# Gated cross-attention block on one core: the opening put in another order, tile 0 normalised by VectorE, first z in one block

## The chip, the cores and the metric

The kernel runs on 1 core of a Trainium2 chip. The metric is the device time of one execution in microseconds. Engines are named TensorE (PE in the rows; PEld its weight loads; PEldq its queue's own instructions), VectorE (DVE), ScalarE (ACT), GpSimd (POOL) and SyncE (SP, which here only issues DMAs).

## What is computed

x is 2048 tokens of 512 numbers. Each token belongs to one of four experts by its token id, and an expert is one 512 x 512 matrix, ctx[e], used three times. Then a feed-forward block with 1536 inner columns and weights rounded to 8-bit floats follows. Shapes and helper code are left out:

```python
e_id = minimum(clip(itok, 0, 24999) // 6250, 3)
n = layernorm(x)                                  # per token, eps 1e-5
for e in range(4):
    z = n @ ctx[e].T
    h = silu(z) * z
    y = where(e_id == e, h @ ctx[e].T, y)
x = x + tanh(g_xattn) * y
w8 = lambda w: w.astype(float8_e4m3fn).astype(float32)
n = layernorm(x)
fuse = silu(n @ w8(gate_w) * gate_scale) * (n @ w8(up_w) * up_scale)
x = x + tanh(g_ffn) * (fuse @ w8(down_w) * down_scale)
```

## The kernel before

**Stages.** The opening (0 to 17 us) sorts the tokens by expert with one-hot products (lines 971 to 1006 on VectorE, 1396 to 1419 on TensorE), so that 16 tiles of 128 sorted tokens follow each other. GpSimd gathers each tile of x by its row numbers (`gather`, L524). Then 19 steps (16 tiles, and one more for each of the three tiles at which the expert can change) run the expert part: z = tile times matrix (`product_z`), h = z silu(z) on VectorE (`product_h`), h turned by four small TensorE products (`turn_h`, L1391), y = h times matrix (`product_y`), and the sum into x on VectorE (`add_expert`, L1112). Which expert and which tile a step works on is read from three words of a table, `walk` (`load_word`, L370). From 135 us on, four groups of four tiles run the feed-forward block; its 36 weight slabs are rounded during the steps, mostly by GpSimd (L620, L623).

**Precision.** Every operand of z and y is split in a 16-bit high and low part. z has 12 products of 512 columns: high x high and high x low for each of four chunks of 128 rows, and low x high for four. The same holds for y (8 at L1483, 4 at L1487). The high part of a turned tile is a copy by ScalarE (`x_high`, L728), the low part is a difference by VectorE (`x1_low`, L1083).

**Expert 0.** Its matrix is turned by TensorE in the opening (`first_turn`, L1405) into four PSUM banks, MT_FIRST. ScalarE makes the high parts (`first_high`, L705), VectorE the low parts (`first_low`, L1012). The other three matrices are split on ScalarE, VectorE (L1172) and GpSimd (`expert_low(2)`, L595) and turned by DMA. Each matrix is scaled by a power of two taken from its sum of squares: ScalarE sums (`squares`), TensorE adds over the partitions, and VectorE computes in `expert_scales` (L939 to L951) one column for each expert: m_scale, m_inv, z_scale, h_scale and m_inv2; `expert_y_scales` makes y_scale from m_inv2 and m_inv. `hot_steps` compares the expert of each step with 0 to 3; `zh_tables` multiplies this one-hot by the scales and adds over the experts, which gives one scale a step for silu and for h.

**Layer norm.** For each tile VectorE takes statistics (`tile_stats`, L1062), `aggregate` (L1071) and `prepare` (L965, L967), GpSimd raises to the power -1/2 and multiplies (`ln_scalars`, L532, L535), ScalarE normalises into the only buffer xn (`normalise`, L723), and TensorE turns it (`turn_x`, L1391).

**Order.** Each engine has its own list of instructions, written out by hand, and works it in order; semaphores are the only coupling. What stands late in a list is late whatever it waits for. TensorE's list in the opening is: two chunks of first_turn, the sort products, the sum for expert 0, two chunks of first_turn, 16 products whose result nobody reads (L1425), turn of tile 0, the three words, then step 0: eight products of z, turn of tile 1, the sum for experts 1 and 2 (L1463, L1465), four products of z. A step s from 1 on is: turn of tile s+1, z(s), turn of h(s-1), y(s-2), with y(0) and y(1) ahead of the turn of h. Banks: Z alternates between 0 and 5, turned tiles between 2 and 4, turned h is bank 1, y bank 3, small things bank 6.

## Time and profile before

| | us |
|---|---|
| median of 3 runs | 401.99 (401.97 to 402.08) |
| the profiled execution | 401.0 |
| its span | 399.3 |
| TensorE busy | 378.4 (95%) |
| VectorE busy | 224.1 (56%) |
| ScalarE busy | 185.5 (46%) |
| GpSimd busy | 163.2 (41%) |

The page splits the span in 40 equal slices of 10 us; a digit is the busy share of TensorE in a slice in tenths, the second line is the clock that it was granted:

```profile
PE   3889899999999999999999999999999999999992
PEclk9999999999999999999999999999999999999997
```

Only the first slice, those from 10 to 50 us, and the last are below 9 tenths: the first 50 us are the part of the kernel with which the change deals. Of the chain of work that ended last, 79% of the span is TensorE. Times are counted from the start of the span.

### The profile page before, as it was taken

What the parts mean: (1) busy time and instruction counts of PE and PEld (TensorE: products, weight loads), DVE (VectorE), ACT (ScalarE), POOL (GpSimd) and SP (SyncE); (2) the same over time, 40 slices, a digit from 0 to 9 for tenths busy, and PEclk for the clock granted to TensorE, in tenths of its full rate; (3) what the DMA queues carried; (4) which work ended last, traced back from release to release, by engine and by line L of the source; (5) the groups of instructions that cost most, each with busy time, mean ns of one, the idle gap of its engine ahead of it and who ended that gap; (6) DMA issues with size and microseconds to landing.
All of it is one profiled execution on the core that took longest, in us unless ns stands there. A gap on an engine that the chain in (4) does not pass through costs nothing.

```text
span 399.3 us, 6082 instructions
## 1 busy us (share of the span) xinstructions
PE 378.4 (95%) x1920; PEld 184.3 (46%) x1920; DVE 224.1 (56%) x467; ACT 185.5 (46%) x297; POOL 163.2 (41%) x204
## 2 busy tenths in 40 slices
PE   3889899999999999999999999999999999999992
PEld 2444455555545544444444444444444444444460
DVE  5878979998787696787434222224222225322253
ACT  3779457789778428693432222222222222222220
POOL 4778889999999831411008000006200004400003
PEclk9999999999999999999999999999999999999997
DMA  7698684354445340760002000001100000200002
GB/s 263 190 313 183 127 214 113 88 108 114 101 115 112 80 105 2 178 167 0 0 2 79 28 0 0 2 0 54 53 0 0 0 0 28 79 0 2 0 0 105
DMA packets 40075, 29.99 MB, mean 75 GB/s; under 512 B 31192, under 2 KB 31216, under 8 KB 40048
## 3 DMA queue, kind: packets, MB, share of 16 engines
q1 hardware_dynamic: 37488, 21.26, 21.4%
q0 software_dynamic: 2560, 8.39, 6.1%
q8 instruction: 14, 0.23, 0.2%
q14 instruction: 13, 0.11, 0.1%
HBM read 18.11 MB, written 4.19 MB: 56 GB/s over the span
## 4 chain that ended last, share of the span: by engine, by line
PE 79%; DVE 10%; ACT 3%; issue 3%; POOL 2%; DMA 1%; SPq 1%; DVEq 0%; ACTq 0%; POOLq 0%
PE bank L1551 36%; PE bank L1565 17%; PE bank L1467 11%; PE bank L1483 7%; PE bank L1391 3%; PE bank L1487 3%; PE bank L1425 1%; DMA X<-x2rows 1%; DVE xs L1112 1%; DVE stats L1062 1%; DVE W L1278 1%; DVE xs L1372 1%; DVE row_hot L997 1%; DVE X L1369 1%; DVE cs L1289 1%
## 5 line engine op out<-in xcount | busy, mean ns | idle before, releaser
L1551 PE MATMUL bank<-X,W 128*128 (+1 forms) x752 | 170.0, 379 | 0.1
L1551 PEld LDWEIGHTS bank<-X,W 128*128 128x128 bf16 x752 | 73.5, 98 | 88.8 <-ACT late_norms L879 0.6
L1289 DVE SCALAR_TENSOR_TENSOR cs<-bank,up_mul,cs 128x512 f32<-128x512 f32 x47 | 35.3, 751 | 107.1 <-PE bank L1551 102.4
L1565 PE MATMUL bank<-W,cs 128*128 128x512 bf16 x376 | 89.0, 379 | 0.5 <-ACT W L762 0.5
L837 ACT ACTIVATE cs<-bank,gate_mul 128x512 f32<-128x512 f32 x47 | 32.2, 684 | 75.5 <-PE bank L1551 75.5
L844 ACT ACTIVATE cs<-cs 128x512 f16<-128x512 f32 x47 | 29.5, 628 | 79.8 <-DVE cs L1289 79.7
L676 POOL TENSOR_TENSOR xs<-xs,X 128x512 f32<-128x512 f32 x12 | 15.3, 1275 | 125.2 <-DVE X L1369 124.9
L1565 PEld LDWEIGHTS bank<-W,cs 128*128 128x128 f16 x376 | 36.6, 98 | 44.0 <-issue 0.5
L1467 PE MATMUL bank<-M,X 128*128 (+1 forms) x228 | 52.5, 379 | 2.1 <-ACT X L728 1.5
L1315 DVE TENSOR_TENSOR cs<-cs 128x512 f16<-128x512 f32 x47 | 33.7, 716 | 31.4 <-ACT cs L844 31.4
L1483 PE MATMUL bank<-M,hTh 128*128 (+1 forms) x152 | 35.9, 378 | 1.6 <-DVE xs L1112 1.6
L682 POOL DMA_INDIRECT out<-xs,order x16 | 16.7, 1046 | 49.2 <-DVE xs L1372 45.9
L1467 PEld LDWEIGHTS bank<-M,X 128*128 (+1 forms) x228 | 22.2, 98 | 28.1 <-issue 2.9
L623 POOL TENSOR_TENSOR W<-w_sum,w_big 128x512 bf16<-128x512 f32 x21 | 27.1, 1293 | 1.6
L620 POOL TENSOR_TENSOR w_sum<-ws,w_big 128x512 f32<-128x512 f32 x21 | 26.7, 1271 | 0.7
L532 POOL TENSOR_TENSOR ln_tab<-prep,ln_half 128x1 f32<-128x1 f32 (+1 forms) x26 | 16.6, 638 | 19.1 <-DVE prep L967 18.9
L786 ACT ACTIVATE silu_z<-bank,z_step 128x512 f32<-128x512 f32 x18 | 12.3, 686 | 22.2 <-PE bank L1467 20.1
L636 POOL TENSOR_TENSOR x2rows<-x2n,x2rows 128x512 f16<-128x512 f32 x16 | 19.5, 1222 | 7.3 <-ACT x2n L739 7.3
L1483 PEld LDWEIGHTS bank<-M,hTh 128*128 128x128 f16 x152 | 13.6, 97 | 16.6 <-issue 2.6
L747 ACT ACTIVATE w_big<-ws 128x512 f32<-128x512 f32 x36 | 21.3, 627 | 0.0
L1062 DVE BATCH_NORM_STATS2 stats<-xs 128x6 f32<-128x512 f32 x31 | 20.7, 683 | 0.0
L1487 PE MATMUL bank<-M,hTl 128*128 (+1 forms) x76 | 19.5, 379 | 0.0
(172 smaller groups left out, 385.6 us busy)
## 6 DMA issues: line engine op xcount, KB each, us to landing
ws<-in_L_ffn_gate_w SPq DMA_DIRECT2D x12, 256.0 KB, 2.6
ws<-in_L_ffn_up_w SPq DMA_DIRECT2D x12, 256.0 KB, 3.2
ws<-in_L_ffn_down_w SPq DMA_DIRECT2D x12, 256.0 KB, 2.9
cs<-in_ctx SPq DMA_DIRECT2D x2, 1024.0 KB, 6.7
X<-in_ctx SPq DMA_DIRECT2D x2, 1024.0 KB
xs<-in_x,order POOLq DMA_INDIRECT x16, 4.2
dsc<-in_L_ffn_down_scale SPq DMA_DIRECT2D x1, 256.0 KB
X<-x2rows SPq DMA_TRANSPOSE x16, 3.1
```

Of the source, the lines that this page charges most:

```text
L620: g.tensor_tensor(w_sum[:], ws[:, slot], w_big[:, slot], ALU.add).then_inc(sum_done, 1)
L623: g.tensor_tensor(dst, w_sum[:], w_big[:, slot], ALU.subtract).then_inc(q_done, 1)
L837: a.activation(sg[:, c % 2, :], GATE[c % 2][:], ACT.Silu, scale=gate_mul[:, c:c + 1]).then_inc(sg_done, 1)
L844: a.activation(fuse_part(g, c, 0), fuse[:, c % 2, :], ACT.Copy).then_inc(fh_done, 1)
L1062: return v.bn_stats(stats[:, slot, which, :], xs_tile(tile))
L1289: v.scalar_tensor_tensor(out=fuse[:, c % 2, :], in0=UP[c % 2][:], scalar=up_mul[:, c:c + 1], in1=sg[:, c % 2, :], op0=ALU.mult, op1=ALU.mu ...
L1315: v.tensor_tensor(fuse_part(g, c, 1), fuse[:, c % 2, :], fuse_part(g, c, 0), ALU.subtract).then_inc(fl_done, 1)
L1467: ins = t_.matmul(Z[lo % 2][:], lhs, rhs, start=(n == 0), stop=(n == 3 * KC - 1))
L1483: t_.matmul(Y[:], hTh[:, lo % 2, k * P:(k + 1) * P], expert_block(e, part, k), start=(k == 0 and part == 0), stop=False)
L1487: ins = t_.matmul(Y[:], hTl[:, lo % 2, k * P:(k + 1) * P], expert_block(e, 0, k), start=False, stop=(k == KC - 1))
L1551: ins = t_.matmul(dst[c % 2][:].rearrange("p (t i) -> p t i", t=TPG), w, x2_group(g, part, k), start=(k == 0 and part == 0), stop=(k == KC ...
L1565: ins = t_.matmul(ACC[t][:], fuse_part(g, c, part)[:, t * P:(t + 1) * P], W8[:, down_slab(c), :], start=(c == 0 and part == 0), stop=(c == ...
```

## The change

On ScalarE, `normalise(0)` goes. On VectorE, a TENSOR_SCALAR with mean and factor as scalars makes xn of tile 0 instead, between the low part of chunk 1 and the statistics of tile 1; the low parts of chunks 2 and 3 come behind the statistics of tile 1. On TensorE the first word is loaded ahead of the turn of tile 0, the second and third in steps 3 and 4 behind the turn of h. The first z has the order high x high (four), high x low (four), low x high (four), waits for the low parts only ahead of the second four, and isn't interrupted; the turn of tile 1 and the sum for experts 1 and 2 follow it. The turned chunks 0 and 2 of expert 0 exchange their banks, so that bank 0, in which the first z is built, is free once chunk 0 is split. In step 2 the turns of the two scale rows and the sum for expert 3 go ahead of y(0). On VectorE, m_inv2 is computed in `expert_y_scales`, with a wait behind it; in step 2 `add_expert(0)` goes ahead of the scales of expert 3, the tables follow these at once, and the y scale comes behind h_low(1). A second copy of the one-hot, HOT, is written to PSUM (bank 7), and `zh_tables` reads that one.

```diff
@@ -192,12 +192,13 @@
         Z = [bank[0], bank[5]]
         XT = [bank[2], bank[4]]
         HT, Y, M0_SUM, SMALL = bank[1], bank[3], bank[4], bank[6]
-        MT_FIRST = [bank[5], bank[7], bank[0], bank[1]]
+        MT_FIRST = [bank[0], bank[7], bank[5], bank[1]]
         ACC = [bank[0], bank[1], bank[2], bank[3]]
         GATE = [bank[5], bank[7]]
         UP = [bank[6], bank[4]]
 
         M_SUM = 192
+        HOT = bank[7][:, 0:E * STEPS].rearrange("p (e s) -> p e s", e=E)
 
 
         consts = sem("consts")
@@ -228,6 +229,7 @@
         msum_done = sem("msum_done")
         mchain = sem("mchain")
         mscale_done = sem("mscale_done")
+        minv2_done = sem("minv2_done")
         mT_done = sem("mT_done")
         mhi_done = sem("mhi_done")
         stats_done = sem("stats_done")
@@ -767,7 +769,6 @@
             squares(1, 0, KC, 1, 1)
             first_high()
             squares(2, 0, KC // 2, 2, 2)
-            normalise(0)
             act.wait_ge(params_in, 64)
             a.activation(tgx[:], gx[:], ACT.Tanh).then_inc(tanh_done, 1)
             a.activation(tgf[:], gf[:], ACT.Tanh).then_inc(tanh_done, 1)
@@ -947,8 +948,8 @@
                                      ALU.logical_shift_left), mchain, mcount)
                 link(v.reciprocal(m_inv[:, c], m_scale[:, c]), mchain, mcount)
                 v.tensor_scalar(z_scale[:, c], m_inv[:, c], 1.0 / X_SCALE, None, ALU.mult)
-                v.tensor_scalar(h_scale[:, c], m_scale[:, c], 2.0 ** -24 / X_SCALE, None, ALU.mult)
-                v.tensor_tensor(m_inv2[:, c], m_inv[:, c], m_inv[:, c], ALU.mult).then_inc(mscale_done, 1)
+                v.tensor_scalar(h_scale[:, c], m_scale[:, c], 2.0 ** -24 / X_SCALE, None,
+                                ALU.mult).then_inc(mscale_done, 1)
 
             def expert_y_scales(i, lo, hi):
 
@@ -958,6 +959,8 @@
                     v.tensor_scalar(tgx24[:], tgx[:], 2.0 ** 24, None, ALU.mult).then_inc(gates_done, 1)
                     dve.wait_ge(gates_done, 1)
                 dve.wait_ge(mscale_done, 2 + i)
+                v.tensor_tensor(m_inv2[:, c], m_inv[:, c], m_inv[:, c], ALU.mult).then_inc(minv2_done, 1)
+                dve.wait_ge(minv2_done, 1 + i)
                 v.scalar_tensor_tensor(out=y_scale[:, c], in0=m_inv2[:, c], scalar=tgx24[:, 0:1], in1=m_inv[:, c],
                                        op0=ALU.mult, op1=ALU.mult).then_inc(ys_done, 1)
 
@@ -1051,7 +1054,10 @@
             prepare(0, 0, 1)
             dve.wait_ge(sort_v, chained[0])
             v.tensor_copy(walk[:], e_words[:]).then_inc(walk_done, 1)
-            first_low(range(1, KC))
+            first_low([1])
+            dve.wait_ge(ln_chain, 1)
+            v.tensor_scalar(xn[:], xs[:, 0, :], mv[:, 0, 0, 0:1], ln_tab[:, 0, 0, 0:1], ALU.subtract,
+                            ALU.mult).then_inc(xn_done, 1)
 
             def slab_big(n, slot):
 
@@ -1086,15 +1092,16 @@
             dve.wait_ge(gathered[1], 32)
             tile_stats(1, 0, 1).then_inc(stats_done, 1)
             aggregate(1, 1, 0, 1)
+            first_low(range(2, KC))
             x1_low(0)
 
             def zh_tables(i, experts, steps):
 
                 n = steps.stop - steps.start
                 dve.wait_ge(mscale_done, 2 + i)
-                dve.wait_ge(step_hot_done, 1)
+                dve.wait_ge(step_hot_done, 2)
                 for part, scales in enumerate((z_scale, h_scale)):
-                    ins = v.tensor_tensor(step_sel[:, part, 0:experts, steps], step_hot[:, 0:experts, steps],
+                    ins = v.tensor_tensor(step_sel[:, part, 0:experts, steps], HOT[:, 0:experts, steps],
                                           scales[:, 0:experts].unsqueeze(2).to_broadcast([P, experts, n]), ALU.mult)
                 ins.then_inc(step_sel_done, 1)
                 dve.wait_ge(step_sel_done, 1 + i)
@@ -1187,6 +1194,9 @@
 
             def hot_steps():
                 v.tensor_tensor(step_hot[:], e_of[:, 0:STEPS].unsqueeze(1).to_broadcast([P, E, STEPS]),
+                                iota_q[:, 0:E].unsqueeze(2).to_broadcast([P, E, STEPS]),
+                                ALU.is_equal).then_inc(step_hot_done, 1)
+                v.tensor_tensor(HOT, e_of[:, 0:STEPS].unsqueeze(1).to_broadcast([P, E, STEPS]),
                                 iota_q[:, 0:E].unsqueeze(2).to_broadcast([P, E, STEPS]),
                                 ALU.is_equal).then_inc(step_hot_done, 1)
 
@@ -1212,9 +1222,9 @@
                     x1_low(3)
                 if lo == 2:
                     round_stats(1, 1)
+                    add_expert(0)
                     expert_scales(E - 1, E)
-                    expert_y_scales(1, E - 1, E)
-                    add_expert(0)
+                    zh_tables(1, E, slice(E - 1, STEPS))
                 if lo == 3:
                     expert_low(3)
                     h_low(s - 1, lo - 1)
@@ -1233,7 +1243,7 @@
                     add_expert(s - 2)
                     ffn_norms(0, 2)
                 if lo == 2:
-                    zh_tables(1, E, slice(E - 1, STEPS))
+                    expert_y_scales(1, E - 1, E)
                     v.tensor_copy(gs[:], SMALL[:, 160:160 + IC])
                     v.tensor_copy(us[:], SMALL[:, 176:176 + IC]).then_inc(scales_done, 1)
                 if lo in (5, 6):
@@ -1425,6 +1435,8 @@
                 t_.matmul(XT[0][:], row_hot[:, 0, :], row_hot[:, 0:KC, :].rearrange("p c i -> p (c i)"),
                           start=True, stop=True)
             pe.wait_ge(order_done, 1)
+            words = walk_words(pe)
+            load_word(t_, words, 0)
             pe.wait_ge(xn_done, 1)
             transpose4(XT[0], xn, xT_done)
 
@@ -1434,14 +1446,13 @@
                     return M[:, e, part, k, :]
                 return M[:, ds(e, 1), part, k, :].rearrange("p a f -> p (a f)")
 
-            words = walk_words(pe)
-
             def z_operands(s, lo):
 
                 e = expert_of(words, s) if lo else 0
                 tile = (s - e) & (TILES - 1)
                 return e + 1, [(x_tile(tile, lhs, k), expert_block(e, rhs, k))
-                        for lhs, rights in ((0, (0, 1)), (1, (0,))) for k in range(KC) for rhs in rights]
+                        for lhs, rights in (((0, (0, 1)), (1, (0,))) if lo else ((0, (0,)), (0, (1,)), (1, (0,))))
+                        for k in range(KC) for rhs in rights]
 
             def turn_x(tile):
                 if tile >= 2:
@@ -1450,20 +1461,18 @@
                 transpose4(XT[tile % 2], xn, xT_done)
 
             def product_z(s, lo, matrices, operands):
-                pe.wait_ge(m_ready, matrices)
+                if lo:
+                    pe.wait_ge(m_ready, matrices)
+                else:
+                    pe.wait_ge(mhi_done, KC)
                 pe.wait_ge(xhi_done, min(s + 1, TILES))
                 if lo >= 2:
                     pe.wait_ge(h_done, s - 1)
                 for n, (lhs, rhs) in enumerate(operands):
+                    if lo == 0 and n == KC:
+                        pe.wait_ge(m_ready, 1)
                     if n == 2 * KC:
                         pe.wait_ge(xlo_done, min(s + 1, TILES))
-                    if lo == 0 and n == 2 * KC:
-                        turn_x(1)
-                        pe.wait_ge(ssq_done, 4)
-                        t_.matmul(SMALL[:, M_SUM + 1:M_SUM + E - 1], ones32[:], part_ssq[:, 1:E - 1], start=True,
-                                  stop=False)
-                        t_.matmul(SMALL[:, M_SUM + E - 2:M_SUM + E - 1], ones32[:], part_ssq[:, E:E + 1], start=False,
-                                  stop=True).then_inc(msum_done, 1)
                     ins = t_.matmul(Z[lo % 2][:], lhs, rhs, start=(n == 0), stop=(n == 3 * KC - 1))
                 ins.then_inc(z_done, 1)
 
@@ -1493,12 +1502,15 @@
                 if 1 <= lo < E:
                     turn_x(s + 1)
                 product_z(s, lo, *z_next[0])
+                if lo == 0:
+                    turn_x(1)
+                    pe.wait_ge(ssq_done, 4)
+                    t_.matmul(SMALL[:, M_SUM + 1:M_SUM + E - 1], ones32[:], part_ssq[:, 1:E - 1], start=True,
+                              stop=False)
+                    t_.matmul(SMALL[:, M_SUM + E - 2:M_SUM + E - 1], ones32[:], part_ssq[:, E:E + 1], start=False,
+                              stop=True).then_inc(msum_done, 1)
                 if E <= lo < TILES - 1:
                     turn_x(s + 1)
-                if lo in (2, 3):
-                    product_y(s - 2, lo - 2)
-                if lo >= 1:
-                    turn_h(s - 1, lo - 1)
                 if lo == 2:
                     pe.wait_ge(params_in, 64)
                     pe.wait_ge(mscale_done, 2)
@@ -1506,14 +1518,20 @@
                               stop=True)
                     t_.matmul(SMALL[:, 176:176 + IC], us_rows[:], ident[0:IC, 0:IC], is_transpose=True, start=True,
                               stop=True)
-                for n in squared_of(s - 1, lo - 1) if lo >= 1 else ():
-                    norms(n, n, n % 2, SMALL, KC * n)
-                if lo < STEPS - 1:
-                    z_next[0] = z_operands(s + 1, lo + 1)
                 if lo == 2:
                     pe.wait_ge(ssq_done, E + 1)
                     t_.matmul(SMALL[:, M_SUM + E - 1:M_SUM + E], ones32[:], part_ssq[:, E - 1:E], start=True,
                               stop=True).then_inc(msum_done, 1)
+                if lo in (2, 3):
+                    product_y(s - 2, lo - 2)
+                if lo >= 1:
+                    turn_h(s - 1, lo - 1)
+                for n in squared_of(s - 1, lo - 1) if lo >= 1 else ():
+                    norms(n, n, n % 2, SMALL, KC * n)
+                if lo in (3, 4):
+                    load_word(t_, words, lo - 2)
+                if lo < STEPS - 1:
+                    z_next[0] = z_operands(s + 1, lo + 1)
                 if lo >= 4:
                     product_y(s - 2, lo - 2)
 
@@ -1527,8 +1545,6 @@
                     ins = t_.matmul(out_col, sq[:, slot, j * P:(j + 1) * P], ones[:, 0:1], start=True, stop=True)
                 ins.then_inc(norm_done, 1)
 
-            for i in range(WORDS):
-                load_word(t_, words, i)
             z_next = [z_operands(0, 0)]
             for s in range(STEPS):
                 step(s, s)
```

## Rows read from the trace of the kernel before

**Rows 1.** Windows view, one stage: length, then busy us of each engine.

```profile
80.00:110.00 30.00, 29.99 (x184) 16.55 (x183) 25.79 (x52) 25.07 (x44) 28.27 (x30) 1.00 0.47 108
```

**Rows 2.** Waits of TensorE: line, awaited, us in total, times, longest.

```profile
PE bank L1483 <- DVE xs L1112: 1.6, 3, 1.0
...
PE bank L1565 <- ACT W L762: 0.5, 1, 0.5
```

**Rows 3.** Timeline of TensorE: start, us, line, operation, [idle before <- releaser].

```profile
11.82 5.65 PE L1425 MATMUL bank<-row_hot 128*128 128x512 f16 x16
...
17.31 0.60 PE L1391 MATMUL bank<-ident,xn 128*128 128x128 f32 x4
...
19.37 1.89 PE L1467 MATMUL bank<-M,X 128*128 128x512 f16 x8 [1.46 <-ACT X L728]
...
21.09 0.60 PE L1391 MATMUL bank<-ident,xn 128*128 128x128 f32 x4
...
21.89 1.02 PE L1467 MATMUL bank<-M,X 128*128 128x512 f16 x4
...
46.47 0.66 PE L1391 MATMUL bank<-ident,h 128*128 128x128 f32 x4 [1.33 <-DVE h L1185]
...
55.71 2.75 PE L1467 MATMUL bank<-M,X 128*128 x12
```

**Rows 4.** Timeline of VectorE, 15 to 46 us.

```profile
15.11 2.06 DVE L1012 SCALAR_TENSOR_TENSOR M<-bank,m_scale,M 128x512 f16<-128x512 f32 x3
...
18.59 0.68 DVE L1083 TENSOR_TENSOR X<-bank,X 128x512 f16<-128x512 f32 x1
...
22.36 0.69 DVE L1083 TENSOR_TENSOR X<-bank,X 128x512 f16<-128x512 f32 x1 [1.87 <-issue]
...
34.90 0.16 DVE L939 TENSOR_SCALAR m_sum<-bank 128x1 f32<-128x1 f32 x1 [0.32 <-PE bank L1515]
...
35.99 1.02 DVE L951 TENSOR_TENSOR m_inv<-m_inv 128x1 f32<-128x1 f32 x1
...
37.04 1.07 DVE L961 SCALAR_TENSOR_TENSOR y_scale<-m_inv,tgx 128x1 f32<-128x1 f32 x1
...
38.04 0.74 DVE L1112 SCALAR_TENSOR_TENSOR xs<-bank,y_step,xs 128x512 f32<-128x512 f32 x1
...
39.96 0.46 DVE L1097 TENSOR_TENSOR step_sel<-step_hot,z_scale 128x64 f32<-128x64 f32 x1
...
40.94 0.16 DVE L1237 COPY gs<-bank 128x12 f32<-128x12 f32 x1
...
41.09 0.41 DVE L1059 TENSOR_SCALAR w_big<-w_big 128x512 f32<-128x512 f32 x1
...
45.67 0.74 DVE L1185 SCALAR_TENSOR_TENSOR h<-bank,h_step,silu_z 128x512 f32<-128x512 f32 x1
```

**Rows 5.** Timeline of ScalarE, 16 to 23 us.

```profile
16.09 0.81 ACT L723 ACTIVATE xn<-xs,ln_tab 128x512 f32<-128x512 f32 x1 [1.10 <-POOL ln_tab L535]
...
17.95 0.60 ACT L728 ACTIVATE X<-bank 128x512 f16<-128x512 f32 x1 [0.86 <-PE bank L1391]
...
22.22 0.80 ACT L723 ACTIVATE xn<-xs,ln_tab 128x512 f32<-128x512 f32 x1
```

**Rows 6.** TensorE's queue by source line: count, ns min/median/max, first and last start.

```profile
L370 PEldq TENSOR_LOAD <-walk x3: 304/324/496, 17.1 to 18.6; - x3
...
L1467 PEldq FUSED_REGOPS  x26: 46/46/83, 53.6 to 61.8; - x26
```

**Rows 7.** Timeline of GpSimd, 15 to 41 us.

```profile
15.20 0.58 POOL L532 TENSOR_TENSOR ln_tab<-prep,ln_half 128x1 f32<-128x1 f32 x1 [0.51 <-DVE prep L967]
...
20.87 0.58 POOL L532 TENSOR_TENSOR ln_tab<-prep,ln_half 128x1 f32<-128x1 f32 x1
...
35.84 4.50 POOL L595 TENSOR_TENSOR W<-X,W 128x512 f16<-128x512 f32 x4 [0.29 <-issue]
...
40.29 0.56 POOL L532 TENSOR_TENSOR ln_tab<-prep,ln_half 128x1 f32<-128x1 f32 x1
```

## The prediction

> **What bounds the kernel now.** First the windows view, for how full TensorE is in each stage: 29.99 of 30 us busy between 80 and 110 [rows 1]. Most of the span is therefore TensorE's own work, none of which the change touches: a saving has to come from an idle stretch of TensorE, or from the 16 useless matmuls ahead of the first tile. Then its waits: in the opening 1.46 us on ScalarE's copy of the first turned tile and 1.33 us on h of step 3 (in brackets behind the instruction that waited [rows 3]), 1.6 us in three waits for a sum into x by VectorE, of which 1.0 stands before y of step 1 and about 0.5 near 141 us, and 0.5 on a slab near 169 us [rows 2]. The timeline shows what stands ahead of each. The last two waits of the opening are one story: VectorE goes from one instruction to the next without a pause from 34.90 to 46.41, and TensorE turns h of step 3 at 46.47, right behind it [rows 3, 4]. From there TensorE is full, so the end of the kernel moves as y of step 2 (47.13, behind those four turns) moves. That instant is what I forecast.
>
> **Tile 0 normalised by VectorE.** ScalarE now makes xn from 16.09 to 16.90 [rows 5]. The 16 filler matmuls run from 11.82 to 17.47, and the turns of tile 0 begin at 17.31, as the last filler drains [rows 3]. The change leaves the 16 alone, so an earlier xn is hidden by them: worth 0. Cover lost: none, since xn on VectorE is due by 17.3. It waits for the first of GpSimd's two table instructions (15.20 and 0.58 [rows 7], so 15.8), follows one chunk of first_low (2.06/3 = 0.69 us, from 15.11), and costs 0.41 (the 128x512 f32 TENSOR_SCALAR of L1059) to 0.74 us (a SCALAR_TENSOR_TENSOR of that size) [rows 4]: it ends between 16.3 and 16.6. I take 0.41, the same operation, though nothing depends on it.
>
> **First z.** Between the copy of turned tile 0 (ends 18.55) and z (19.37) lie 0.8 us in which TensorE's queue loads the three words of the walk: they start from 17.1 to 18.6, (18.6 - 17.1)/2 = 0.75 us each [rows 3, 5, 6]. Two move to steps 3 and 4; the first moves ahead of the wait for xn. Whether it then delays the turns depends on how far that queue runs ahead. The address work for a z whose matmuls begin at 55.71 [rows 3] is done from 53.6 [rows 6], some 2 us ahead; and walk is written just before the first_low of 15.11. Cost 0, at most the 0.75 if it had to wait for the fillers. The Trainium skill ("TensorE: Matmul & The Clock Gate", Specifications) gives TensorE's queue as 64 deep; by it the 16 fillers all fit in the queue, and the load is hidden too. So z starts at about 18.7. Its first four products need high parts alone and end at 19.6. The low parts of chunks 2 and 3 now follow tile 1's statistics on VectorE: these start between 16.6 and 17.17 (where 15.11 + 2.06 let them start before), take 1.42 with their aggregate and prepare (17.17 to 18.59 [rows 4]), then 2 x 0.69 gives 19.4 to 20.0; x1_low(0) adds 0.6. The other eight products run at 0.22 each from there: z ends at 21.4 (21.3 to 21.8), against 22.9 before (1.02 from 21.89 [rows 3]).
>
> **What is late next.** z(0) is consumed by silu(0), which stands behind x_high(1) and normalise(2) on ScalarE, and these hang on turn_x(1). That began at 21.09 in the middle of z and now stands behind the whole of it: 21.3 to 21.6. So the gain of 1.5 us on z ends here, and tile 1 comes 0.05 to 0.4 us later; I take 0.1. Besides, tile 2's statistics are now behind two chunks and x1_low(0) on VectorE: its prepare ends about 21.4, and GpSimd's pow, which began at 20.87 [rows 7], begins near 21.5 and gives ln_tab near 22.5. normalise(2), at 22.22 [rows 5], waits for that, so z(1) comes about 0.4 late. GpSimd's gathers 5 and 6 behind it slip by 0.6 too; they are wanted by statistics after 30 us, which covers that. Z(1)'s delay is mostly hidden again: ScalarE's next steps (the 2 us copy of expert 1, x_high(2), normalise(3)) hang on the scales of experts 1 and 2, behind x1_low(1) on VectorE (22.36 [rows 4]), plus 0.1 and less 0.07 for the m_inv2 taken out. I carry +0.1 on ScalarE's chain (0 to 0.4), and with it on GpSimd's expert_low(2), which starts at 35.84 because ScalarE's scaled rows do. VectorE itself, without a pause from 23 us on, gets the second one-hot (0.15), m_inv2 with its wait in the y scales (0.2) and the 0.1: it reaches the end of round_stats(1) 0.4 late, at 34.9.
>
> **Steps 2 and 3.** The sum of squares of expert 3 is taken three us earlier, so VectorE's wait of 0.32 us [rows 4] goes. add_expert(0) goes ahead of the scales: x1 of tile 0 is ready at 35.6 instead of 38.78, and the 1.0 us that TensorE waits for it [rows 2] goes. That gain is then lost at the next wait, for h of step 3, unless VectorE comes earlier as well. There the four GpSimd instructions of expert_low(2), 4.50/4 = 1.12 us each from 35.84 to 40.34 [rows 7], decide. m_inv2 took 1.02 us and y_scale 1.07 for one column, and ended at 37.01 and 38.11, where GpSimd's first and second instruction ended [rows 4, 7]; each waited for GpSimd. The Trainium skill ("SBUF — State Buffer", Who interferes with whom) says the same: an instruction with two SBUF inputs waits for a GpSimd one that reads SBUF, one with an input in PSUM doesn't; by that rule the PSUM copy frees step_sel of the 0.46 against 0.22 [rows 4], and leaves m_inv2 and y_scale to pay. They are moved, not freed. In the new order VectorE has from 34.9: add_expert 0.66, seven small ones 1.1, the tables 0.95, product_h(2) 0.66, h_low(1) 0.6, and m_inv2 is issued at 38.9. That is inside GpSimd's third instruction (38.2 to 39.3), y_scale falls into the fourth, and ends at 40.34 + 0.1 = 40.45, later than in the old order. Behind y_scale VectorE had 46.41 - 38.04 = 8.37 us of work; of it add_expert, product_h, h_low and the tables, 40.94 - 38.04 = 2.90, now go before. So h of step 3 ends at 40.4 + 0.1 + 5.47 = 45.95. If w_big, which took 0.41 us at 41.09, is held by GpSimd's pow (40.29, 0.56 us), 0.45 more: 46.4. Middle 46.2, that is 0.2 earlier than 46.41.
>
> **The moved words.** Word 1 is loaded in step 3, and TensorE idles anyway for h of step 3 one z and one turn later: 0; that idle (1.33 us before, more now) is the cover. Word 2 is loaded between the turns of h(3) and y(2), just behind that wait, where the queue has had no time to run ahead. The turns take 0.66 [rows 3], the load 0.75: 0.05 to 0.3 exposed, I take 0.15.
>
> **Sum.** -0.2 + 0.15 = about 0. The profiled execution took 401.0 us (399.3 span and 1.7 around it), 1.0 under the median of 401.99, so the difference is put on the median: 401.99 - 0.05, 401.9. Its own range: -0.46 (nothing held, load hidden) with the opening's -0.1, to +0.3 (w_big held, load exposed) with +0.3: 401.4 to 402.6.
>
> **Rivals.** (1) The change does nothing that the end sees, TensorE's gaps merely trade places: 402.0. For it speaks the filler cover and the merge at h(3); it differs from the forecast by its reason. (2) The shift is kept and the late waits go too. 0.5 + 0.5 us are left after 120 us [rows 2]; they rest on VectorE and ScalarE chains whose phase against GpSimd may change. With 0.2: 401.99 - 0.2 - 0.95 = 400.85. Against it: those chains follow TensorE. (3) m_inv2 is issued before GpSimd's second instruction ends (38.2): y_scale ends 1.12 earlier, 401.9 - 1.1 = 400.8. It needs VectorE 0.7 us quicker than worked out. (4) The slower side: tile 1 slips by 0.4, VectorE issues m_inv2 after 39.3, so it takes GpSimd's fourth instruction and y_scale the pow behind it (40.4 to 41.0). y_scale ends at 41.1 in place of 40.45, +0.6; with the slip's other 0.3 and 0.15 more of the load, 401.9 + 1.05 = 402.95. It decides from 0.4 us of lateness on VectorE on.
>
> **Chances.** Forecast 0.56, (1) 0.12, (2) 0.10, (3) 0.07, (4) 0.15. The measurement tells about 0.2% (0.8 us: 401.19 to 402.79) from nothing. Faster is (2) and (3), 0.17; slower is (4), 0.15; same is the rest, 0.68. The range from 401.0 to 403.0 leaves out (2) and (3) alone.
>
> **What would show it.** Turns of tile 0 at 17.3 to 17.5 again (else the load blocks); z(0) in one block from about 18.7; turn_x(1) at 21.3 to 21.6; normalise(2) near 22.6; no wait for add_expert(0), but one near 1.8 us for h of step 3; m_inv2 and y_scale about 1.6 us in sum, y_scale ending with expert_low(2); y(2) at 47.1 within 0.4. I am wrong if the turns of tile 0 start later, if y_scale ends before 39.5 or after 41, or if the stretch after 120 us has another idle sum than 1 us.

## The result, and the profile after

The changed kernel took 403.91 us, the median of eight executions (403.04 to 405.07), against 401.99 (eight, 400.85 to 402.14). The ratio is 1.0053, with a 95% interval of 1.0035 to 1.0071: slower by more than the 0.2% that the measurement tells apart. Forecast was 401.9, with a range of 401.0 to 403.0. The profiled execution took 404.73, its span is 403.0, against 401.0 and 399.3 of before. 3.7 us of span are to be found. That is twice the 1.9 us between the medians: the profiled execution of before is one of its fastest, that of after one of its four slowest.

The page's slices of 10 us, TensorE's busy share and its granted clock:

```profile
PE   3889799999999999999999999999999999999992
PEclk9969999999999999999999999999999999999998
```

The third slice has a clock of 6 where before had a 9: TensorE worked there at a lower clock. The fifth slice is less full, 7 for 8. The windows view, for TensorE, cuts this finer (length, busy us, granted clock, DMA share, GB/s). First after, then before:

```profile
20.00:24.00 4.00, 4.00 (x16) 0.57 0.92 334
24.00:28.00 4.00, 2.56 (x13) 0.88 1.02 395
28.00:32.00 4.00, 4.00 (x18) 0.69 0.31 94
...
50.00:120.00 70.00, 69.05 (x410) 1.00 0.54 123
```

```profile
20.00:24.00 4.00, 3.54 (x22) 1.00 0.97 300
24.00:28.00 4.00, 3.57 (x20) 1.00 1.02 393
28.00:32.00 4.00, 3.71 (x19) 1.00 0.69 163
...
50.00:120.00 70.00, 69.84 (x415) 1.00 0.49 122
```

Two things differ. The granted clock is 1.00 in these stretches of before; after it is 0.57, 0.88 and 0.69 in the three from 20 to 32 us. And 0.8 us of idle time are new between 50 and 120 us. What follows is only shifted: a wait that stood at 141.95 us stands at 145.68, 3.7 later. TensorE's timeline names both (start, us, line, operation, idle before and its releaser), as [rows 3] does for before:

```profile
11.83 4.40 PE L1435 MATMUL bank<-row_hot 128*128 128x512 f16 x16
16.31 0.66 PE L1401 MATMUL bank<-ident,xn 128*128 128x128 f32 x4
17.75 1.02 PE L1476 MATMUL bank<-M,X 128*128 128x512 f16 x4 [0.78 <-ACT X L730]
19.88 3.29 PE L1476 MATMUL bank<-M,X 128*128 128x512 f16 x8 [1.10 <-DVE M L1015]
...
25.38 0.63 PE L1401 MATMUL bank<-ident,xn 128*128 128x128 f32 x4 [1.14 <-DVE X L1089]
26.31 4.45 PE L1476 MATMUL bank<-M,X 128*128 x12 [0.30 <-issue]
...
49.18 0.66 PE L1401 MATMUL bank<-ident,h 128*128 128x128 f32 x4 [1.97 <-DVE h L1192]
49.94 1.89 PE L1492 MATMUL bank<-M,hTh 128*128 x8
...
81.83 1.89 PE L1492 MATMUL bank<-M,hTh 128*128 x8 [0.95 <-DVE xs L1119]
```

The row of y of step 2 in the kernel before:

```profile
46.96 1.89 PE L1483 MATMUL bank<-M,hTh 128*128 x8
```

The eight products of the first z behind the pause of 1.10 us took 3.29 us in place of 1.89 [rows 3], the twelve of the second z 4.45 in place of the 2.75 that twelve take at full clock [rows 3]: the lower of the two levels, 1.2 GHz for 2.4. y of step 2 begins at 49.94, where it began at 46.96: 2.98 us. (The prediction's 47.13 is 46.47 + 0.66, the end of the row of the four turns ahead of it; the rows overlap, so starts are compared with starts here.) The last row of after is the other loss: 0.95 us of waiting for add_expert near 81 us, where before waits 0.15 in all between 50 and 120 us. 2.98 + 0.80 = 3.8, for 3.7 of span.

Of the other engines, VectorE around the part of steps 2 and 3 that answers to [rows 4], and GpSimd's row that answers to [rows 7]:

```profile
15.71 0.55 DVE L1059 TENSOR_SCALAR xn<-xs,mv,ln_tab 128x512 f32<-128x512 f32 x1
...
18.42 1.40 DVE L1015 SCALAR_TENSOR_TENSOR M<-bank,m_scale,M 128x512 f16<-128x512 f32 x2
...
39.65 0.22 DVE L1104 TENSOR_TENSOR step_sel<-bank,z_scale 128x64 f32<-128x64 f32 x1
...
41.64 0.97 DVE L962 TENSOR_TENSOR m_inv<-m_inv 128x1 f32<-128x1 f32 x1
42.65 1.08 DVE L964 SCALAR_TENSOR_TENSOR y_scale<-m_inv,tgx 128x1 f32<-128x1 f32 x1
...
48.39 0.73 DVE L1192 SCALAR_TENSOR_TENSOR h<-bank,h_step,silu_z 128x512 f32<-128x512 f32 x1
```

```profile
39.21 4.50 POOL L597 TENSOR_TENSOR W<-X,W 128x512 f16<-128x512 f32 x4 [1.01 <-ACT X L718]
```

The y scale ends at 43.73, with GpSimd's four instructions (43.71), and h of step 3 5.4 us behind it. The step's mechanism is the forecast one; it stands 3 us later because all that feeds it does.

### The profile page after: what moved, and what is told of

The parts are those of the page before. It is cut to its first block, busy times and chain, and to the rows that moved or that the text cites. A ratio compares the mean times of both kernels' runs of the same rounds, so it can differ in the third digit from the quotient of the medians.

```text
span 403.0 us, 6081 instructions
## 1 busy us (share of the span) xinstructions
PE 380.6 (94%) x1920; PEld 185.1 (46%) x1920; DVE 223.6 (55%) x468; ACT 184.7 (46%) x296; POOL 163.0 (40%) x204
## 3 DMA queue, kind: packets, MB, share of 16 engines
q1 hardware_dynamic: 37488, 21.26, 21.3%
## 4 chain that ended last, share of the span: by engine, by line
PE 75%; DVE 12%; issue 4%; ACT 4%; POOL 2%; DMA 2%; DVEq 1%; ACTq 0%; POOLq 0%
PE bank L1567 35%; PE bank L1581 17%; PE bank L1476 9%; PE bank L1492 7%; PE bank L1401 3%; PE bank L1496 3%; DVE stats L1068 1%; DMA xs<-in_x,order 1%; DVE xs L1119 1%; DMA X<-x2rows 1%; DVE W L1288 1%; DVE xs L1382 1%; DVE row_hot L1000 1%; DVE X L1379 1%; DVE cs L1299 1%
## 5 line engine op out<-in xcount | busy, mean ns | idle before, releaser
L1476 PE MATMUL bank<-M,X 128*128 (+1 forms) x228 | 55.6, 395 | 2.2 <-DVE M L1015 1.1
L787 ACT ACTIVATE silu_z<-bank,z_step 128x512 f32<-128x512 f32 x18 | 12.4, 689 | 24.0 <-PE bank L1476 22.6
L749 ACT ACTIVATE w_big<-ws 128x512 f32<-128x512 f32 x36 | 21.3, 626 | 0.3 <-issue 0.3
L1492 PEld LDWEIGHTS bank<-M,hTh 128*128 128x128 f16 x152 | 13.6, 97 | 16.3 <-issue 2.2
L1192 DVE SCALAR_TENSOR_TENSOR h<-bank,h_step,silu_z 128x512 f32<-128x512 f32 x18 | 13.5, 748 | 11.8 <-PE bank L1401 6.8
```

Source lines behind the costliest of these rows:

```text
L749: a.activation(w_big[:, slot], ws[:, slot], ACT.Abs, scale=FP8_STEP).then_inc(abs_done, 1)
L1476: ins = t_.matmul(Z[lo % 2][:], lhs, rhs, start=(n == 0), stop=(n == 3 * KC - 1))
L1492: t_.matmul(Y[:], hTh[:, lo % 2, k * P:(k + 1) * P], expert_block(e, part, k), start=(k == 0 and part == 0), stop=False)
```

## The experiments

The theory has two prices. First the clock: the new order puts pauses of TensorE next to each other in the opening, behind them it is granted the lower level, and that costs 1 to 1.7 us each time. Second the order itself, at full clock. Rivals: the order alone (the clock is a bystander), or the clock alone. Every run was timed in five rounds beside the kernel before on the same chip, which gave 401.98 to 402.07 each time (29 to 35 executions in the first three groups, 17 in the last). These fall into three clusters; in the second group, 5 of 34 took 400.88 to 401.00, 22 took 401.87 to 402.11, and 7 took 403.19 to 403.76, these at a mean clock of 0.991 to 0.993. So the kernel before has a slow cluster of its own, which its eight executions beside the changed kernel happened not to show. An unread product is a product of 512 columns whose result nobody reads; it keeps TensorE busy for 0.22 us.

**Filling the pauses of the opening.**

```diff
 # kernel after: behind the turn of tile 0, ahead of the second four
 # products of z(0), and behind the sum for experts 1 and 2
+for i in range(3):  # 4, 5 in the other places
+    t_.matmul(Y[:], row_hot[:, 0, :], ..., start=True, stop=True)
```

> The changed kernel with 12 more products that nobody reads (128x512, bank 3), 3 behind the turn of tile 0, 4 behind the first four products of z(0), 5 behind the sum for experts 1 and 2: they stand where TensorE idled in the changed kernel (0.8, 1.1 and 1.1 us). Theory A (the loss is TensorE's clock, granted 0.50 from about 20 to 23.5 and from 27 to 30.5 us, behind these pauses): the granted clock stays 1.00 up to 50 us, z(0) and z(1) run at 0.22 us a product, y of step 2 starts between 46.9 and 47.6 and the time comes back to 401.4 to 402.6. Theory B (the loss is the order: tile 1, the statistics of tile 2 and the scales are late whatever the clock): y of step 2 stays above 49 us and the time at 403.5 to 405.

403.14 (402.11 to 404.76), ratio 1.0020 [1.0000, 1.0039]. The median lies between the ranges of theory A (to 402.6) and theory B (from 403.5). In the profiled execution (402.19, span 400.4) the clock was 1.00 in every stretch, and the two z are back at full speed:

```profile
19.87 1.90 PE L1482 MATMUL bank<-M,X 128*128 128x512 f16 x8
...
24.80 2.76 PE L1482 MATMUL bank<-M,X 128*128 x12 [0.48 <-issue]
...
46.61 0.66 PE L1401 MATMUL bank<-ident,h 128*128 128x128 f32 x4 [2.07 <-DVE h L1192]
47.46 1.89 PE L1498 MATMUL bank<-M,hTh 128*128 x8 [0.19 <-issue]
```

17.75 to 19.88 and 26.31 in after, 17.91 to 19.87 and 24.80 here: the first z begins and resumes where it did, and what follows is earlier because it runs at full speed. y(2) comes 2.5 us earlier, inside theory A's range, though TensorE does 12 products more. That is the clock's share between these two executions. The wait of 0.9 near 79 us stays, and so does the wait of 2 us for h(3). Five of the twelve executions still have a mean clock of 0.989 to 0.993; that they fell behind this wait is likely from the experiments below, but no trace of one shows it.

**Four more fillers ahead of tile 0.**

```diff
-            for i in range(16):
+            for i in range(20):
```

> The changed kernel with 20 instead of 16 unread products ahead of the turn of tile 0, so that this turn comes about 0.9 us later and z(0) finds its low parts 0.2 us and not 1.1 us away. Theory A, with the pause inside z(0) as what lets the clock fall: the clock stays 1.00 in the profile, 401.5 to 402.7. Theory A with the pause behind the sum for experts 1 and 2 (1.1 us) as the other cause: one stretch at 0.50 is left, about 1.7 us, 402.8 to 404. Theory B: later still than the changed kernel, 404 to 405.5.

403.34 (402.71 to 404.39), 1.0031 [1.0014, 1.0048]. The first z is then one block at full clock, but the pause for x of tile 1 stands, and the second z is slow:

```profile
19.36 2.75 PE L1476 MATMUL bank<-M,X 128*128 128x512 f16 x12 [0.78 <-ACT X L730]
...
24.02 0.63 PE L1401 MATMUL bank<-ident,xn 128*128 128x128 f32 x4 [1.14 <-DVE X L1089]
24.96 4.45 PE L1476 MATMUL bank<-M,X 128*128 x12 [0.31 <-issue]
```

In this trace one pause fewer saves one fall, not the other. The twelve times agree with falls that come singly: two executions took 402.7 to 402.8 at a mean clock of 0.996 to 0.997, seven 403.2 to 403.4 at 0.991 to 0.992, three 404.3 to 404.4 at 0.985.

**Each part of the change alone.** The opening and the moved words alone (steps 2 and 3 undone), and the part of steps 2 and 3 alone, put into the kernel before:

```diff
 # opening_only: kernel after with
-                    add_expert(0)
                     expert_scales(E - 1, E)
-                    zh_tables(1, E, slice(E - 1, STEPS))
+                    expert_y_scales(1, E - 1, E)
+                    add_expert(0)
 # and m_inv2, HOT and TensorE's sum for expert 3 as before;
 # steps_only: the reverse of these edits in the kernel before
```

> The changed kernel with its part in steps 2 and 3 undone (m_inv2, the second one-hot in PSUM, add_expert(0) ahead of the scales, the sum for expert 3 ahead of y(0)); the opening and the moved words stay. Theory A puts the whole loss in the opening: the stretches at half clock are there, 403.3 to 405.5, at most 0.5 us above the changed kernel since the part in steps 2 and 3 is worth 0 to 0.5. Theory B: the same. A third theory, that the part in steps 2 and 3 costs the time: 401.5 to 402.3.

> The kernel before with the part in steps 2 and 3 alone. From the prediction's own steps: y_scale again ends with GpSimd's fourth instruction of expert_low(2), TensorE no longer waits before y(1), h of step 3 comes 0 to 0.5 us earlier, no word is loaded there: 401.4 to 402.1. If the part in steps 2 and 3 costs the time: 403 or more. The clock stays 1.00 in the profile by every theory.

The opening alone: 402.93 (402.65 to 406.77), 1.0039 [1.0013, 1.0065]; executions at a clock of 0.994 to 0.996 took 402.65 to 402.97, those at 0.988 to 0.989 405.0, at 0.984 406.75. The median is below the 403.3 that both theories wanted: most executions had no fall, and the loss that is left in them is the order's. The steps alone: 402.36 (401.63 to 403.75), 0.9999 [0.9982, 1.0017], above the expected 402.1; its four executions at a clock of 0.996 to 0.997 took 401.63 to 401.72. That the clock would stay 1.00 by every theory was wrong. Its trace shows a fall of the clock at another place, right behind the two waits for VectorE that the change merges into one of 2.01 us. TensorE's timeline, and one stretch of the windows view:

```profile
45.91 1.11 PE L1398 MATMUL bank<-ident,h 128*128 128x128 f32 x4 [2.01 <-DVE h L1189]
46.82 3.14 PE L1490 MATMUL bank<-M,hTh 128*128 x8
```

```profile
46.00:50.00 4.00, 4.00 (x13) 0.58 0.59 110
```

The granted clock was 0.58. Eight products of y took 3.14 in place of 1.89. So the opening's part makes a loss by itself, and the steps' part gives back behind its longer wait what it gains ahead of it. A fall doesn't come in each execution: the profiled one of the opening alone (402.69, span 400.9) had the clock at 1.00 behind pauses of 0.78 and 1.14 us; there the fillers ended late, at 17.4, and the first z was nearly one block:

```profile
18.60 3.02 PE L1471 MATMUL bank<-M,X 128*128 128x512 f16 x12 [0.78 <-ACT X L730]
21.46 0.60 PE L1396 MATMUL bank<-ident,xn 128*128 128x128 f32 x4
...
47.99 1.89 PE L1487 MATMUL bank<-M,hTh 128*128 x8 [0.49 <-issue]
```

This trace shows the order's price with neither a fall nor an unread product more than before: y(2) at 47.99 for 46.96, 1.03 us, and waits for add_expert of 0.26 and 0.47 us at 66.8 and 79.8 where before has 0.15, together the 1.6 us of its span.

The length of a pause alone doesn't decide whether the clock falls. Behind pauses of 1.10 and 1.14 us in after, 1.14 in fillers_20 and 2.01 in steps_only it fell; behind 1.14 in opening_only, 1.65 in steps_only, 1.97 in after and 2.07 in fill_gaps it didn't. What else does, no run here shows.

**All pauses filled, in both kernels.** To take the clock out of the comparison:

```diff
 # kernel before: 6 behind the turn of tile 0, 4 ahead of y(1),
 # 5 ahead of the turn of h(3)
 # kernel after: as in the first experiment, and ahead of the turn of h(3)
+                if lo == 4:
+                    pe.wait_ge(zh_tables_done, 2)
+                    for i in range(8): t_.matmul(bank[7][:], ...)
```

> The kernel before with 15 products that nobody reads where TensorE idles: 6 behind the turn of tile 0, 4 ahead of y(1), 5 ahead of the turn of h(3). Theory (the executions of the kernel before at 402.0, 402.5 and 403.6 us are those in which the clock fell behind one of these pauses, and 401.0 is the one in which it didn't): nearly every execution comes at 400.9 to 401.4, median about 401.1, the mean clock 0.994 or more. If the spread has another cause: the median stays at 402 with the same spread.

> fill_gaps with 8 more unread products ahead of the turn of h(3), where TensorE still waits 2.1 us. Clock theory: the executions at 403.3 to 404.8 of fill_gaps go, the median is 402.1 to 402.4 with hardly a spread, mean clock 0.995 or more; what is left against before_filled is the order's own price, 1.1 us (0.33 at y of step 2, 0.8 in the wait of 0.9 near 78 us). Otherwise the median stays at 403 and over.

The kernel before so filled: 401.04 (400.88 to 401.72), 0.9980 [0.9966, 0.9993], the lowest median of this study, with none of the executions above 403 us that the kernel before has. The kernel after so filled: 402.40 (402.12 to 403.31), 1.0018 [1.0005, 1.0030]. With the pauses filled, at mean clocks of 0.993 to 0.997 in all executions of both, the change still loses 402.40 - 401.04 = 1.36 us, 1.2 of span (400.3 against 399.1). Against the kernel before as it is, 401.98, the loss is only 0.4, for the filling takes 0.94 us off the kernel before as well. So the order has its own price, and it has two parts. The first, in TensorE's timeline of the filled kernel after:

```profile
47.31 1.45 PE L1498 MATMUL bank<-M,hTh 128*128 x6
```

y(2) starts at 47.31 against 46.84 in the filled kernel before, 0.47 us; and the wait of 0.95 us for add_expert near 79 us, against 0.15 near 72, gives the other 0.8.

**Where the words are loaded.**

```diff
-                if lo in (3, 4):
-                    load_word(t_, words, lo - 2)
+                if lo == 3:
+                    load_word(t_, words, 1)
+                    load_word(t_, words, 2)
```

> after_filled with words 1 and 2 both loaded in step 3, ahead of the wait for h of step 3, none in step 4. y of step 2 then follows the turns of h(3) at once, 0.2 us (opening_only showed up to 0.5) earlier. Phase theory (the 0.9 us wait near 78 us comes because VectorE's prepare is issued just after GpSimd's instruction begins, not just before it, for want of 0.3 us): the shift may be enough to make it go: 401.2 to 401.4; if it stays: 401.9 to 402.1. If the load isn't what delays y(2): 402.1 to 402.4 as after_filled.

402.50 (401.67 to 403.25), 1.0017 [1.0007, 1.0027]: the same, and a miss of all three expectations. The loads now expose 0.54 us ahead of z(4), y(2) stays at 47.30. The run doesn't isolate the load at y(2): z(4) is later, so the eight unread products behind it keep TensorE until the turns of h(3) begin at 46.86, though h(3) is ready at 46.58. The wait of 0.95 at 79 us is gone, but 0.42 are waited at 127.6 us instead, and the span is 400.3 again. This called for a test of the late waits by themselves.

**A delay that does nothing else.** In the kernel before, in its filled form, and in the filled form with the steps' part, two unread products between the turn of h(3) and y(2), 0.43 us:

```diff
+                if lo == 4:
+                    for i in range(2): t_.matmul(bank[7][:], ...)
                 if lo >= 4:
                     product_y(s - 2, lo - 2)
```

> The kernel before with 2 unread products (0.43 us) between the turn of h(3) and y(2), nothing else. If a delay of TensorE there costs just itself: its undisturbed executions come at 401.4. Phase theory: VectorE's work after it is late against GpSimd's rounding, which isn't, and a wait of 0.5 to 1 us for a sum into x appears between 70 and 85 us: undisturbed executions at 401.9 to 402.4.

> The filled kernel before with 2 more products that nobody reads between the turn of h(3) and y(2): 0.43 us of delay there, all else equal and the clock kept full. A delay that only adds: 401.04 + 0.43, so 401.3 to 401.6. If the shift of TensorE's phase against VectorE and GpSimd near 80 us is what costs, as in the same delay without the filling: 401.8 to 402.3, with a wait of 0.8 to 1.0 for the sum into x near 80 us.

The first: 402.12 (401.97 to 403.83), 1.0007 [0.9991, 1.0022], with a wait of 0.93 us at 80.6 that its kernel had not, though the profiled execution (403.50) also had a fall of the clock in the opening, behind a pause of 1.71 us ahead of the first z (eight products in 2.89 us for 1.89; granted 0.50 to 0.52 from 20 to 23 us). That opening is the one of the kernel before, so this is probably what its cluster at 403.19 to 403.76 is. The second has no fall and is the clean case: 402.16 (402.02 to 402.79), against 401.04 without the two products (on another chip; the kernel before took 401.98 on the one, 402.00 on the other). 0.43 us of delay cost 1.12 us. VectorE and GpSimd show why. Filled, without the delay, and then with it (timeline of both engines):

```profile
75.45 0.16 DVE L965 SCALAR_TENSOR_TENSOR prep<-mv,ln_mul 128x2 f32<-128x2 f32 x1
75.50 1.26 POOL L623 TENSOR_TENSOR W<-w_sum,w_big 128x512 bf16<-128x512 f32 x1
75.53 1.25 DVE L967 SCALAR_TENSOR_TENSOR prep<-mv,ln_mul 128x2 f32<-128x2 f32 x1
76.70 0.42 DVE L1059 TENSOR_SCALAR w_big<-w_big 128x512 f32<-128x512 f32 x1
...
77.03 0.74 DVE L1112 SCALAR_TENSOR_TENSOR xs<-bank,y_step,xs 128x512 f32 x1
```

```profile
75.69 1.27 POOL L623 TENSOR_TENSOR W<-w_sum,w_big 128x512 bf16<-128x512 f32 x1
75.89 1.08 DVE L965 SCALAR_TENSOR_TENSOR prep<-mv,ln_mul 128x2 f32<-128x2 f32 x1
76.89 0.15 DVE L967 SCALAR_TENSOR_TENSOR prep<-mv,ln_mul 128x2 f32<-128x2 f32 x1
76.91 1.16 POOL L636 TENSOR_TENSOR x2rows<-x2n,x2rows 128x512 f16<-128x512 f32 x1
76.97 1.39 DVE L1059 TENSOR_SCALAR w_big<-w_big 128x512 f32<-128x512 f32 x1
...
78.28 0.74 DVE L1112 SCALAR_TENSOR_TENSOR xs<-bank,y_step,xs 128x512 f32 x1
```

Without the delay the first small instruction of VectorE (L965) comes 0.05 us ahead of GpSimd's slab instruction and only the second is held, until 76.7; w_big then runs unhindered in 0.42. With the delay the first one comes 0.20 behind GpSimd's start and is held until that ends, and so w_big meets GpSimd's next instruction and is held too, 1.39. The sum into x starts at 78.28 for 77.03: 1.25 us late for 0.43 of delay, and TensorE waits 0.95 for it at 79.16. The filled kernel after shows the same rows: `prep` for 1.07 at 75.93, w_big for 1.39 at 76.99, the sum at 78.31.

**Each part of the change at full clock.**

```diff
 # steps_filled: the filled kernel before, with the steps' part,
 # and 8 products for 4 + 5, held until the tables of expert 3
 # opening_filled: opening_only, filled: 3, 4, 5 as above, 4 ahead of y(1), 5 ahead of h(3)
```

> Kernel before with 15 products that nobody reads (6 behind the turn of tile 0 and, held until the tables of expert 3 are made, 8 ahead of the turn of h(3), in place of 4 and 5), and with the part of the change that lies in steps 2 and 3 (add_expert first, m_inv2 in the y scales, tables at once, second one-hot in PSUM, sum for expert 3 ahead of y(0)). No word load moves, the opening stays. Clock theory: what the steps' part alone lost was the clock behind the merged 2.0 us wait, so this is as the filled kernel before, 400.9 to 401.3. Order theory: y scale ends no earlier, and the shift of VectorE against GpSimd costs without any clock: 401.6 to 402.2, with a wait of 0.8 to 1.0 for the sum into x near 80 us.

> Kernel after with the part in steps 2 and 3 undone, and 21 products that nobody reads in the pauses (3 behind the turn of tile 0, 4 inside the first z, 5 behind the sum for experts 1 and 2, 4 ahead of y(1), 5 ahead of the turn of h(3)): the opening and the moved words alone, without the clock. If the opening's order makes the loss by itself (tile 1 late by 0.3 to 0.4, word 2 exposed by 0.5, sum 0.9 at y(2)): 401.9 to 402.5, y(2) near 47.7. If the clock was all of it: 400.9 to 401.3.

The opening's part: 402.93 (402.69 to 404.04), 1.0031 [1.0016, 1.0046], y(2) at 47.97, both above what either expectation gave, and the same as in the undisturbed executions of opening_only. That is 1.13 us behind the filled kernel before: its turn of h(3) starts at 47.21 for 46.34 (0.87), and 0.26 are the exposed load of word 2. The steps' part, with 14 unread products: 401.60 (400.73 to 401.72), 0.9985 [0.9974, 0.9996], the low end of the order theory. Here y(2) begins at 46.53, 0.31 us earlier than in the filled kernel before, and yet the span is 399.9 for 399.1. TensorE's timeline shows the wait, though not near 80 us:

```profile
91.25 1.89 PE L1493 MATMUL bank<-M,hTh 128*128 x8 [0.95 <-DVE xs L1116]
```

The same two engines near 88 us, in the filled kernel before and with the steps' part:

```profile
88.06 0.16 DVE L965 SCALAR_TENSOR_TENSOR prep<-mv,ln_mul 128x2 f32<-128x2 f32 x1
88.09 1.27 POOL L623 TENSOR_TENSOR W<-w_sum,w_big 128x512 bf16<-128x512 f32 x1
```

```profile
87.78 1.27 POOL L625 TENSOR_TENSOR W<-w_sum,w_big 128x512 bf16<-128x512 f32 x1
88.02 1.05 DVE L969 SCALAR_TENSOR_TENSOR prep<-mv,ln_mul 128x2 f32<-128x2 f32 x1
```

0.03 us ahead of GpSimd costs nothing, 0.24 behind it 0.95. One of its twelve executions took 400.73, 0.85 less than the rest, at the same clock; I read it as one that met no such row, but that execution has no trace. Of the 0.8 us of span, 0.95 - 0.31 = 0.64 are so placed, 0.16 are not.

> The steps' part with 14 filling products, and 2 more between the turn of h(3) and y(2): y(2) begins 0.43 us later, near 46.97, where it stands in the kernel before, in place of 46.53. If a delay of TensorE adds to the time: 401.6 + 0.43, 402.0. If what costs is where VectorE's prepare for the layer norm falls against GpSimd's slab instruction (0.24 us behind its start near 88 us in the run without the delay, 0.03 us ahead of it in the filled kernel before): the delay puts it ahead again, the 0.95 us wait near 91 us goes, and the time is 401.6 + 0.43 - 0.95 = 401.1 or less, faster although it does more. It can also fall behind another slab instruction, near 76 us; then 401.9 to 402.1 with a wait there.

With the delay of two products on top: 401.86 (401.64 to 403.08), 0.9994 [0.9979, 1.0009]. The last branch of the expectation came: the wait at 91 us goes. But GpSimd's instruction at 75.38 now starts 0.23 ahead of VectorE's (75.61), and TensorE waits 0.93 us at 78.85. One collision was exchanged for another, so the kernel with the steps' part was not made faster than the filled kernel before.

## Why the prediction was wrong

**The missing term: the clock of TensorE.** This is the step that failed first of all: the prediction's sum has no term for it, and gives none of the pauses that the new order makes a price beside its length. It measured 2.5 us at y(2) in the profiled executions, and 1.5 between the medians of the changed kernel unfilled and filled (403.91 and 402.40). Its list of signs names idle sums and starting times, not a product that takes twice as long. Before, the pauses of the opening were 1.46 us, then short ones [rows 3]; the new order leaves 0.78, 1.10 and 1.14 us between 17 and 25.4 us. Gaps that "merely trade places", as rival (1) has it, can change the clock between them. Of the 1.9 us between the medians, what the clock makes differs from one execution to the next: 403.04 to 403.33 in four of eight (clock 0.989 to 0.992), 404.49 to 405.07 in the other four (0.985 to 0.988). The Trainium skill ("TensorE: Matmul & The Clock Gate", Part 1: The HAM clock gate) describes a gate with two levels that depends on the recent activity of TensorE and that is not tied to the start of a kernel. The trace agrees with the two levels (granted 0.50 and 1.00, products 0.425 and 0.216 us apart), and the spread from one execution to the next agrees with the rest.

**Tile 0 normalised by VectorE.** "The change leaves the 16 alone, so an earlier xn is hidden by them" takes their end for fixed. They are 16 products in both kernels, but took 4.40 us for 5.65 [rows 3] and ended at 16.2. That isn't the change's doing: in the thirteen traces with 16 of them they took 4.08 to 5.65 us, 4.12 to 5.65 with the old opening and 4.08 to 5.56 with the new one. The first of them are 0.425 us apart, the later ones 0.216, and how many are slow differs. So the turns of tile 0 started at 16.3, not at 17.3 to 17.5, a miss by the prediction's own test. xn was ready by then (15.71 + 0.55, at the bound of 16.3). With ScalarE's xn a short run of fillers doesn't help as much, as the trace of steps_filled shows: its fillers took 4.12 us, and the turns of tile 0 began at 16.95, after 1.01 us of waiting for xn. So of the 1.0 us, about 0.6 (16.95 - 16.31) is the worth of the earlier xn when the fillers are short; it is nothing when they are long. The next step ate it.

**First z.** Forecast: z starts at about 18.7, its first four products end at 19.6, the low parts come at 19.4 to 20.0. The low parts came at 19.82, but z began at 17.75. Its four high products were through 1.1 us before the low parts were there. The block was split by a wait, and that pause is the one with the fall behind it. The prediction had its two numbers side by side (19.6, and up to 20.0) and gave the pause no price. Where the fillers were long, in opening_only, its opening came as forecast: z at 18.60 and nearly in one block, the turn of tile 1 at 21.46, normalise(2) at 22.59, and no fall.

**What is late next: right in kind, mis-sized.** In the filled kernel after, turn_x(1) is at 21.57 (forecast 21.3 to 21.6), z(0) ends at 21.7, normalise(2) starts at 22.70 (forecast near 22.6). But I carried +0.1 us to ScalarE and GpSimd, out of 0 to 0.4. In the filled kernels expert_low(2) starts at 36.58 for 35.71: 0.87. The turn of tile 1 stands 0.6 later (21.57 for 20.97), and nothing in the chain behind it took any of that back. In opening_only, against the kernel before, both are 0.37 later (21.46 for 21.09, 36.21 for 35.84), the upper end of the range. A part of the difference is the filling itself, which is not free here: from the turn of tile 1 to z(1) it is 3.19 us in the filled kernel after and 3.01 in opening_only. The waits that I took for cover stood themselves behind the delayed tile.

**Steps 2 and 3: right, but for the clock.** With the clock full and the opening as before, the y scale ended at 40.59 (forecast 40.45), with GpSimd's four instructions (36.07 + 4.51 = 40.58), and h(3) at 45.98 (forecast 45.95 to 46.4). m_inv2 took 0.85 and y_scale 1.08; rival (3), m_inv2 inside GpSimd's second instruction, came in no run. As forecast, the wait for add_expert(0) is gone and one of 2.0 us stands before h(3). step_sel with an input in PSUM took 0.22 for 0.46 [rows 4], while y_scale with both inputs in SBUF was held for 1.08. The Trainium skill ("SBUF — State Buffer", Who interferes with whom) has this rule, and this trace agrees. The gain at y(2) was 0.31 (forecast 0.2). What was not foreseen is that behind this merged wait the clock falls in some executions.

**The moved words.** Word 0 is hidden, as said. Word 2: y(2) starts 0.49 us behind the turns of h(3) in before, 0.76 in after, after_filled and opening_filled, 0.85 in fill_gaps and 1.15 in opening_only, so the load exposes 0.27, 0.36 and 0.66 us (forecast 0.05 to 0.3, 0.15 in the sum). Word 1 is free.

**Rival (2) and rival (4).** Rival (2) held that late waits may go because of VectorE's phase against GpSimd. The waits of 0.46 and 0.45 us behind 120 us stayed, but a shift against GpSimd did change a late wait, with the opposite sign and at another place: 0.8 us came near 80 us. I had weighed it as a gain only, against a trace of before in which that phase happened to be right (0.07 us ahead at 75.57), and the signs of being wrong watched only the stretch behind 120 us. Rival (4), the slower side (402.95), named the lateness of tile 1 and the loads, and its place and price (0.87 and 0.26) are close to what the opening's part costs at full clock, 402.93. That its number fits is luck: it laid the loss to m_inv2 meeting another GpSimd instruction, which happened in no run.

**The account.** Filled against filled: opening 0.87 + 0.26, steps' part -0.66 behind it (h(3) turned at 46.55 in the filled kernel after, 47.21 without the steps' part), together 0.47 at y(2), then 0.8 in the late wait, 1.2 of span with -0.1 unplaced. The 1.5 from 402.40 to 403.91 go to the clock. But 1.36 + 1.5 counts from 401.04, the filled kernel before; the kernel before as it is stands at 401.98 and has 0.94 of loss of its own, so that the difference measured is 1.9. What is open: the kernel before itself has executions near 400.95 and, more of them, near 402.0, at the same mean clock of 0.993 to 0.997. The step of 1.0 is the size of one such late wait, and its filled form stays at 401.0; no trace of an execution of 402.0 was at hand, so this isn't shown.

## What to carry to other kernels

A pause of an engine with a gated clock has a second price beside its length: before pauses are moved next to each other or merged, cost the work behind them at half speed, and try to fill them with products that nobody reads. Here this took 0.94 us off even the kernel before (401.04 for 401.98), though how much of that is the clock isn't shown. When a small shift early in a kernel changes a stage far behind it, look for two engines that lock each other out: find the pair of rows that start within 0.3 us of each other, and take the price of either order as part of the range. And where a step rests on cover that ends at a time read from one trace (fillers at 17.47 us), ask what set that end.

## What the runs showed that I had not expected

- Behind pauses of 1.10 and 1.14 us the clock was granted at 0.50 (products at 0.425 in place of 0.216 us, in blocks of 3.3 to 4.5 us), in some executions and not in others. Products added to such pauses cost at most 0.2 us and took 2.5 us off.
- The 16 fillers, the same instructions at the same start, took 4.08 to 5.65 us from one execution to the next, in both kernels. The profile's granted clock reads 1.00 in all of that stretch, also where they are 0.425 us apart.
- A delay of 0.43 us at 47 us of the kernel cost 1.12 us at its end; an advance of 0.31 us cost 0.6 to 0.8. The rows that decide lie 0.05 us ahead or 0.20 behind one another.
- Loading a word from SBUF into a register on TensorE's queue costs 0.27 to 0.66 us for one load right behind a wait. In step 3, where TensorE has work ahead, one load is free and two cost 0.54 us.
